# Attention with probabilities in two 16-bit planes: four DMA transposes per block in place of TensorE transposes

## The chip, the cores and the metric

The kernel runs on one core of a Trainium2 chip. The metric is device time in microseconds (us). Three timed runs of the kernel before gave 1548.31, 1543.1 and 1545.7 us, median 1545.7. Engines are named as in the profile: PE (TensorE, matmuls), PEld (its weight loads), DVE (VectorE), ACT (ScalarE), POOL (GpSimd), and SP, which issues the DMAs.

## The reference, cut to what matters

Two layers of attention and feed-forward; the change touches only the attention of the first layer. Batch is 8, with 256 own and 256 context positions, width 512, 16 query heads and 4 key/value heads of 128.

```python
q = rms_norm((x @ wq), q_norm_w)          # 16 heads; x has been layer-normalised
k = rms_norm((x @ wk), k_norm_w); v = x @ wv
k_ctx = rms_norm(h_ctx_kv @ wk_ctx, k_norm_w); v_ctx = h_ctx_kv @ wv_ctx
q = q * cos + rotate_half(q) * sin;  k = k * cos + rotate_half(k) * sin
k_full = concat([k_ctx, k]); v_full = concat([v_ctx, v])   # each repeated for 4 query heads
p = softmax(mask(q @ k_full.T / sqrt(128)))                # causal over own positions
out = (p @ v_full) @ wo
```

## The kernel before, in words

Attention is 64 blocks. Block i is one batch (i // 8), one key/value head (i // 2 % 4) and one half of its 128-query tiles (i % 2); it holds four query heads. An even block sees 384 keys (three tiles of 128), an odd one 512 (four tiles), so `width(i)` is 384 or 512 and `tiles_in(i)` is 3 or 4. A group is an even and an odd block that share keys and values. "Unit" u is one half (context for even, own for odd u, but for the first two) of the keys and values of group u // 2; unit i + 2 is computed during block i.

Precision is kept by splitting values into a high part and the rest: every product is three matmuls, high by high, low by high, high by low. In one block, in the order of the data: PE multiplies queries and keys into score banks (`pe_s`); DVE adds the mask, scales and takes the negative row maximum (`dve_ev`, L877); ACT takes the exponential and its row sum (`act_exp`, L617); DVE inverts the sums (`dve_ri`, L885); POOL multiplies by them (`pool_norm`, L1135); PE transposes the probabilities per tile of keys, four 128x128 each (`pe_p_turn`, L408); ACT copies the transposed bank as the high part (L609), DVE subtracts for the low part (L862); PE multiplies with the values (`pe_pv`, L421); ACT and DVE split the result into `OT` (L625, L912) and SP stores it (L282).

Beside that runs the preparation of later blocks. Keys and values of unit i + 2: PE (`pe_kv`, L338), ACT squares (`act_k_sq`), DVE adds epsilon (`dve_k_ss`, L800), POOL takes the power -0.5 (`pool_k_rs`, L1106), DVE multiplies (`dve_k_n`, L807), for own keys POOL applies the rotation in four instructions (`pool_k_rope`, L1113 to L1117), PE transposes (`pe_k_turn`), ACT and DVE split into `kT` (L575/L577, `dve_k_lo` L817/L819). Queries of block i + 2 go through `pe_q` (L368), `dve_q` (L841 to L843), `pool_q_add` (L1123), `pool_q_rs` (L1129), `pe_q_turn`, L601 and L855. Once per batch, in its blocks 4 to 6, context and x of the next batch are split, normalised (`dve_ln_a` L778 to L782, `dve_ln_b` L788) and transposed.

The order on each engine is written out by hand (`pe_even`, `pe_odd` and their counterparts); engines meet by counting semaphores, and each engine runs its list strictly in order. So a wait in a list holds all behind it. The first scores of an even block wait for the keys of its group (`kt_lo`, set by `dve_k_lo`) and its queries (`qt_lo`).

After attention PE multiplies with `wo` (`pe_y`, L1356) and the feed-forward follows. Its hidden values are already transposed by DMA (`sp_h_turn`, L1288): a 128x1024 16-bit tile per DMA.

## Time and profile before

| | value |
|---|---|
| profiled execution, its own time | 1547.26 us |
| its span | 1546.0 us, 26210 instructions |
| median of three timed runs | 1545.7 us |
| busy: PE, PEld, DVE, ACT, POOL | 96%, 75%, 74%, 62%, 45% of the span |
| granted clock, mean | 0.993 |
| attention, steady part | from about 100 to 860 us |

The page shows one profiled execution. Busy times are unions over an engine's instructions; matmuls are pipelined, so the time that one takes in a row of matmuls is the distance of the starts (0.23 us for 512 columns), not its own duration (about 0.39 us). An idle time is put down to what released it.

### The profile page before, as it was taken

The numbers are of one execution on the slowest core, as the hardware profiler recorded it, in microseconds if no ns is written. First come the engines' busy times: TensorE is split into PE (matmuls) and PEld (weight loads), VectorE is DVE, ScalarE is ACT, GpSimd is POOL, SyncE is SP. The second block draws the span as 40 slices with busy tenths as digits, with TensorE's granted clock in tenths as the row PEclk, the third lists the DMA queues.
The fourth block names the chain that finished last, engine by engine and source line by source line (L and its number), as shares of the span: only waits on it lengthen the run. The fifth ranks groups of instructions, "written<-read, shape, count | busy, mean of one in ns | idle before, by whom it ended". The sixth has DMA issues, their size and how long they took to land. (4 is left out here: it accounts for less than half of the span.)

```text
span 1546.0 us, 26210 instructions
## 1 busy us (share of the span) xinstructions
PE 1488.8 (96%) x8644; PEld 1165.6 (75%) x8644; DVE 1137.2 (74%) x2966; ACT 959.3 (62%) x2470; POOL 692.1 (45%) x832
## 2 busy tenths in 40 slices
PE   7899999999999999999999999999998899999988
...
GB/s 281 28 42 55 42 69 42 42 69 42 56 56 42 69 42 42 69 42 56 57 190 177 263 288 292 260 248 261 260 210 203 99 9 54 56 49 42 28 14 28
DMA packets 84327, 165.09 MB, mean 107 GB/s; under 512 B 39392, under 2 KB 39520, under 8 KB 82784
## 3 DMA queue, kind: packets, MB, share of 16 engines
...
HBM read 113.05 MB, written 41.94 MB: 100 GB/s over the span
## 5 line engine op out<-in xcount | busy, mean ns | idle before, releaser
L617 ACT ACTIVATE Pt<-Pt,small 128x384 f32<-128x384 f32 (+1 forms) x256 | 172.7, 682 | 106.1 <-DVE small L877 106.0
L368 PE MATMUL bank<-wq,xT 128*128 128x512 f32 x768 | 206.7, 404 | 1.0 <-DVE wq L772 1.0
L421 PE MATMUL bank<-PT,vv 128*128 128x512 f32 x672 | 199.6, 405 | 4.7 <-DVE PT L862 3.8
L1135 POOL TENSOR_SCALAR Pt<-Pt,small 128x384 f32<-128x384 f32 (+1 forms) x256 | 164.0, 653 | 79.0 <-DVE small L885 78.9
L877 DVE CUSTOM_DVE_ANT_0 Pt<-quad,mask,small 128x384 f32<-128x384 f32 (+1 forms) x256 | 171.6, 679 | 30.7 <-PE quad L398 29.4
L1356 PE MATMUL bank<-wq,ot 128*128 128x512 f32 x768 | 182.1, 395 | 1.5 <-DMA ot<-ot_scratch 1.5
L862 DVE TENSOR_TENSOR PT<-quad,PT 128x512 fp32r<-128x512 f32 x224 | 153.6, 686 | 37.9 <-ACT PT L609 37.5
L1356 PEld LDWEIGHTS bank<-wq,ot 128*128 128x128 f32 x768 | 143.9, 188 | 33.7 <-DMA ot<-ot_scratch 2.2
L368 PEld LDWEIGHTS bank<-wq,xT 128*128 128x128 f32 x768 | 136.8, 189 | 26.4 <-DVE wq L772 2.3
L1123 POOL TENSOR_TENSOR t<-t 128x512 f32<-128x512 f32 x64 | 83.6, 1306 | 144.1 <-DVE t L843 144.1
L421 PEld LDWEIGHTS bank<-PT,vv 128*128 128x128 f32 x672 | 116.4, 189 | 28.9 <-DVE PT L862 10.2
L1653 POOL TENSOR_TENSOR cl<-cl,fixed 128x1 f32<-128x1 f32 x16 | 8.8, 550 | 276.8 <-DVE cl L1537 276.8
L609 ACT CAST PT<-quad 128x512 fp32r<-128x512 f32 x224 | 128.7, 590 | 6.4 <-PE quad L408 6.4
L408 PE MATMUL quad<-fixed,Pt 128*128 128x128 f32 x896 | 129.0, 272 | 0.9 <-POOL Pt L1135 0.9
L408 PEld LDWEIGHTS quad<-fixed,Pt 128*128 128x128 f32 x896 | 109.2, 140 | 24.3 <-POOL Pt L1135 2.2
L625 ACT CAST OT<-bank 128x512 fp32r<-128x512 f32 x64 | 37.5, 587 | 138.1 <-PE bank L421 138.1
L2539 POOL TENSOR_TENSOR bhw<-bh,lnw 128x512 f32<-128x512 f32 x64 | 81.7, 1277 | 81.9 <-DVE bh L2327 81.9
L396 PE MATMUL quad<-kT,qT 128*128 128x384 f32 (+1 forms) x256 | 99.5, 389 | 2.2 <-DVE small L877 0.8
L1129 POOL TENSOR_TENSOR small<-small,fixed 128x4 f32<-128x4 f32 x64 | 66.1, 1033 | 72.3 <-DVE small L849 72.2
L338 PE MATMUL bank<-wkc,cT 128*128 128x256 f32 x744 | 97.2, 287 | 0.6 <-issue 0.6
L338 PEld LDWEIGHTS bank<-wkc,cT 128*128 128x128 f32 x744 | 91.0, 191 | 8.2 <-DVE vv L828 7.0
L338 PE MATMUL bank<-wkv,xT 128*128 128x256 f32 x744 | 96.5, 286 | 0.0
...
## 6 DMA issues: line engine op xcount, KB each, us to landing
...
```

What stands on the lines that cost most here:

```text
L338: ins = pe.matmul(kv_bank(u)[:, t * 256:t * 256 + 256], src[i][:, k, t * 128:t * 128 + 128], w[j][:, g, k, :], start=(n == 0), stop=(n == 11))
L368: ins = pe.matmul(bQ[:], xT[p][:, k, qt * 128:qt * 128 + 128], wq[j][:, g, k, :], start=(part == 0 and k == 0), stop=(part == 2 and k == 3))
L396: pe.matmul(bank[:, 0:n], qh, kh, start=True, stop=False)
L408: ins = pe.transpose(bP[k % 2][:, h * 128:h * 128 + 128], Pt[i % 2][:, h, kt * 128:kt * 128 + 128], idf[:])
L421: ins = pe.matmul(bO[:], vv[x][:, bg % 2, kt, :], PT[y][:, k % 2, :], start=(kt == 0 and n == 0), stop=(kt == tiles_in(i) - 1 and n == 2))
L609: act.copy(PT[0][:, k % 2, :], bP[k % 2]).then_inc(f["pt_hi"], 1)
L617: act.activation(p, p, ACT.Exp, bias=nm[:, i % 2, h:h + 1], scale=-1.0, accum_out=sm[:, i % 2, h:h + 1]).then_inc(f["s_exp"], 1)
L862: dve.tensor_tensor(PT[1][:, k % 2, :], bP[k % 2], PT[0][:, k % 2, :].bitcast(F32), ALU.subtract).then_inc(f["pt_lo"], 1)
L877: dve.tensor_tensor_reduce(Pt[i % 2][:, h, 0:n], bS[h % 2][:, 0:n], mask[:, 512 - n:512], scale=cq[:, i % 2, h:h + 1], scalar=3.0e38, op0= ...
L1123: pool.tensor_tensor(t1[:], t1[:], t2[:], ALU.add).then_inc(f["q_add"], 1)
L1135: pool.tensor_scalar(p, p, ri[:, i % 2, h:h + 1], 1.0, ALU.mult, ALU.mult).then_inc(f["p_n"], 1)
L1356: ins = pe.matmul(y_bank(n)[:], ot[:, c % 4, i, k * 128:k * 128 + 128].bitcast(F32R), wo[j][:, g, k, :], start=(g == 0 and k == 0 and q == ...
```

## The change

Scores use three banks instead of two (`bank_s`), and the fourth bank of `quad`, once used for transposed probabilities, holds the projections of the even units. The exponentials stay in one buffer `E`. POOL writes the normalised probabilities, times 2 to the 15, as a 16-bit high plane and DVE writes the 16-bit rest beside it; four DMA transposes per block (two heads by two planes) bring them to `PT`. Values are 16-bit planes too, scaled by a factor `sig` per head that is worked out once per batch from sums of squares (`act_c_square`, `pe_scale`, `dve_scale`, `pool_scale`); results are multiplied by `unsig` when they leave PSUM. ACT instead of DVE multiplies the keys (`act_k_n`), POOL instead of DVE applies the layer norm to x (`pool_ln`). The orders of all engines are written anew, one list for even and odd blocks.

```diff
-    bS = [quad[:, 0, :], quad[:, 1, :]]
-    bP = [quad[:, 2, :], quad[:, 3, :]]
+    bS = [quad[:, j, :] for j in range(3)]
...
-    vv = [sb(st, f"vv{j}", [128, 2, 4, 128], F32R) for j in range(2)]
+    vv = sb(st, "vv", [128, 2, 2, 4, 128], F16)
...
-    Pt = [sb(st, "Pt0", [128, 4, 384], F32), sb(st, "Pt1", [128, 4, 512], F32)]
+    E = sb(st, "E", [128, 4, 512], F32)
+    PT = [sb(st, "PT0", [128, 24, 128], F16)]
...
+    planes = sb(st, "planes", [128, 2, 2048], F16)
+    PT.append(sb(st, "PT1", [128, 32, 128], F16))
...
-        return bO if u in (0, 2) else bK
+        return bO if u == 2 else bK if u % 2 else quad[:, 3, :]
...
+    def sp_p_turn(i, p, x):
+
+        n = tiles_in(i)
+        if p == x == 0:
+            after(sp, f["pv_mm"], i - 1)
+        sp.wait_ge(f[("p_n", "p_lo")[x]], 4 * i + 2 * p + 2)
+        sp.dma_start_transpose(PT[i % 2][:, 4 * n * x + 2 * n * p:4 * n * x + 2 * n * p + 2 * n, :],
+                               planes[:, x, 2 * p * width(i):2 * p * width(i) + 2 * width(i)]).then_inc((t_hi, t_lo)[x], 16)
...
+            if i >= 2:
+                p = i - 2
+                sp.wait_ge(f["o_lo"], p + 1)
+                sp.dma_start(ot_dram[2 * (p // 8) + p % 2, p // 2 % 4], OT[:].bitcast(F32)).then_inc(f["ot0"], 16)
...
+            if i < NBLK:
+                for half in range(2):
+                    for x in range(2):
+                        sp_p_turn(i, half, x)
...
-        bank = bS[h % 2]
+        bank = bank_s(i, h)
         if h == 0:
             pe.wait_ge(f["kt_lo"], 2 * bg + 2)
             pe.wait_ge(f["qt_lo"], i + 1)
...
-        after(pe, f["s_ev"], 4 * i + h - 1)
+        if h == 1 and i and scaled(i - 1):
+            pe.wait_ge(f["v_scale"], 3 * scales(i - 1)[0] + 2)
+        after(pe, f["s_ev"], 4 * i + h - 2)
...
-    def pe_p_turn(i, kt):
-        if not 0 <= i < NBLK or kt >= tiles_in(i):
-            return
-        k = tile_of(i, kt)
-        if kt == 0:
-            pe.wait_ge(f["p_n"], 4 * i + 4)
-        after(pe, f["pt_lo"], k - 1)
-        for h in range(4):
-            ins = pe.transpose(bP[k % 2][:, h * 128:h * 128 + 128],
-                               Pt[i % 2][:, h, kt * 128:kt * 128 + 128], idf[:])
-        ins.then_inc(f["pt_mm"], 1)
...
+    def pe_scale(i):
+
+        k, b, lo, n = scales(i)
+        bank = bank_s(i, 2)
+        pe.wait_ge(f["v_sq"], squares(k))
+        pe.wait_ge(f["s_ev"], 4 * i + 3)
+        after(pe, f["v_scale"], 3 * k)
+        for j in range(2):
+            pe.matmul(bank[:, 384:384 + n], ones[:], w_sq[:, j, lo:lo + n], start=(j == 0), stop=(j == 1))
+        for j in range(2):
+            ins = pe.matmul(bank[:, 388:389], ones[:], c_sq[:, j:j + 1], start=(j == 0), stop=(j == 1))
+        ins.then_inc(f["v_scale"], 1)
+
+    def pe_pv(i, part):
+        if i < 0:
+            return
+        n = tiles_in(i)
+        x, y = ((0, 0), (1, 0), (0, 1))[part]
+        if part == 0:
+            pe.wait_ge(f["v_lo"], max(2 * (i // 2) + 2, 3))
             after(pe, f["o_lo"], i)
-        for n, (x, y) in enumerate(PRODUCTS):
-            ins = pe.matmul(bO[:], vv[x][:, bg % 2, kt, :], PT[y][:, k % 2, :],
-                            start=(kt == 0 and n == 0), stop=(kt == tiles_in(i) - 1 and n == 2))
-        ins.then_inc(f["pv_mm"], 1)
+            pe.wait_ge(t_hi, 32 * (i + 1))
+        if part == 2:
+            pe.wait_ge(t_lo, T_LO + 32 * (i + 1))
+        heads = PT[i % 2][:].rearrange("p (x h k) q -> p x h k q", x=2, h=4)
+        for kt in range(n):
+            ins = pe.matmul(bO[:].rearrange("p (h q) -> p h q", h=4), vv[:, x, i // 2 % 2, kt, :], heads[:, y, :, kt, :],
+                            start=(part == 0 and kt == 0), stop=(part == 2 and kt == n - 1))
+        if part == 2:
+            ins.then_inc(f["pv_mm"], 1)
...
         act.wait_ge(f["kt_lo"], u + 1)
-        after(act, f["pv_mm"], 7 * (bg - 1))
-        act.copy(vv[0][:, bg % 2, 2 * own:2 * own + 2, :], kv4(u)[:, 1]).then_inc(f["v_hi"], 1)
+        act.wait_ge(f["v_scale"], 3 * (min(bg, 3) if bg < 4 else bg // 4 + 3) if bg else 3)
+        after(act, f["pv_mm"], 2 * (bg - 1))
+        act.activation(vv[:, 0, bg % 2, 2 * own:2 * own + 2, :], kv4(u)[:, 1], ACT.Copy,
+                       scale=sig[:, bg // 4 % 2, bg % 4:bg % 4 + 1]).then_inc(f["v_hi"], 1)
...
+    def act_k_n(u):
+        if u >= NU:
+            return
+        act.wait_ge(f["k_rs"], u + 1)
+        after(act, f["kt_mm"], u)
+        for t in range(2):
+            ins = act.activation(kn[:, t], kv4(u)[:, 0, t], ACT.Copy, scale=krs[:, t:t + 1])
+        ins.then_inc(f["k_n"], 1)
...
+    def act_c_square(c):
+        b, t = divmod(c, 2)
+        act.wait_ge(f["c_hi"], c + 1)
+        if c in (2, 3):
+            act.wait_ge(f["v_scale"], 7)
+        act_square(c if b == 0 else 8 + c, cT[0][:, :, t * 128:t * 128 + 128], c_sq[:, t:t + 1])
...
-    def dve_k_n(u):
-        if u >= NU:
-            return
-        dve.wait_ge(f["k_rs"], u + 1)
-        after(dve, f["kt_mm"], u)
-        dve.tensor_tensor(kn, kv4(u)[:, 0], krs[:, 0:2].unsqueeze(2).broadcast_to((128, 2, 128)),
-                          ALU.mult).then_inc(f["k_n"], 1)
...
+        vh, vl = (vv[:, j, bg % 2, 2 * own:2 * own + 2, :] for j in range(2))
         dve.wait_ge(f["v_hi"], u + 1)
-        dve.tensor_tensor(vl, kv4(u)[:, 1], vh.bitcast(F32), ALU.subtract).then_inc(f["v_lo"], 1)
+        dve.scalar_tensor_tensor(vl, kv4(u)[:, 1], sig[:, bg // 4 % 2, bg % 4:bg % 4 + 1], vh,
+                                 ALU.mult, ALU.subtract).then_inc(f["v_lo"], 1)
...
-    def dve_p_lo(i, kt):
-        if not 0 <= i < NBLK or kt >= tiles_in(i):
-            return
-        k = tile_of(i, kt)
-        dve.wait_ge(f["pt_hi"], k + 1)
-        dve.tensor_tensor(PT[1][:, k % 2, :], bP[k % 2], PT[0][:, k % 2, :].bitcast(F32),
-                          ALU.subtract).then_inc(f["pt_lo"], 1)
+    def dve_p_lo(i, h):
+
+        dve.wait_ge(f["p_n"], 4 * i + h + 1)
+        if h == 0:
+            after(dve, t_lo, T_LO + 32 * i if i else 0)
+        dve.scalar_tensor_tensor(plane(i, 1, h), E[:, h, 0:width(i)], ri[:, i % 2, h:h + 1], plane(i, 0, h),
+                                 ALU.mult, ALU.subtract).then_inc(f["p_lo"], 1)
...
         dve.wait_ge(f["s_exp"], 4 * i + 2 * p + 2)
-        dve.reciprocal(ri[:, i % 2, 2 * p:2 * p + 2], sm[:, i % 2, 2 * p:2 * p + 2]).then_inc(f["s_ri"], 1)
+        r = ri[:, i % 2, 2 * p:2 * p + 2]
+        v.did(dve.reciprocal(r, sm[:, i % 2, 2 * p:2 * p + 2]))
+        v.settle()
+        dve.tensor_scalar(r, r, FULL, None, ALU.mult).then_inc(f["s_ri"], 1)
```

The new lists of PE, DVE and POOL, cut to what a plain block runs:

```diff
+    def pe_step(i):
+        pe_s(i, 0)
+        pe_s(i, 1)
+        pe_kv(i + 2)
+        pe_s(i, 2)
+        pe_s(i, 3)
+        pe_q_turn(i + 1)
+        for part in range(3):
+            pe_q(i + 2, part)
+        pe_pv(i - 1, 0)
+        pe_pv(i - 1, 1)
+        pe_k_turn(i + 2)
+        pe_pv(i - 1, 2)
...
+    def dve_step(i):
+        dve_ev(i, 0)
+        dve_ev(i, 1)
+        dve_o_lo(i - 2)
+        dve_v_lo(i + 1)
+        dve_q_ve(i + 1)
+        dve_ri(i, 0)
+        dve_last(i, 0)
+        dve_ev(i, 2)
+        dve_k_ss(i + 2)
+        dve_p_lo(i, 0)
+        dve_ev(i, 3)
+        dve_p_lo(i, 1)
+        dve_ri(i, 1)
+        dve_q_lo(i + 1)
+        dve_p_lo(i, 2)
+        dve_p_lo(i, 3)
+        if i % 8 == 5 and i + 3 < NBLK:
+            dve_ln_a(2 * (i // 8) + 2)
+            dve_ln_a(2 * (i // 8) + 3)
+        dve_last(i, 1)
+        dve_k_lo(i + 2)
+        dve_q(i + 2)
...
+    def pool_ln(m):
+        t, x = m % 2, x_slot(m)
         pool.wait_ge(f["ln_var"], m + 1)
-        pool.tensor_tensor(rs[:, t:t + 1], ve[:, t:t + 1], half[:, 0:1], ALU.pow).then_inc(f["ln_rs"], 1)
+        g_.did(pool.tensor_tensor(rs[:, t:t + 1], ve[:, t:t + 1], half[:, 0:1], ALU.pow))
+        g_.settle()
+        pool.tensor_scalar(x, x, mv[:, 2 * t:2 * t + 1], rs[:, t:t + 1], ALU.subtract, ALU.mult).then_inc(f["ln_x"], 1)
...
     def pool_norm(i, h):
-        p = Pt[i % 2][:, h, 0:width(i)]
         if h % 2 == 0:
             pool.wait_ge(f["s_ri"], 2 * i + h // 2 + 1)
-        pool.tensor_scalar(p, p, ri[:, i % 2, h:h + 1], 1.0, ALU.mult, ALU.mult).then_inc(f["p_n"], 1)
+        if h == 0:
+            after(pool, t_hi, 32 * i)
+        pool.tensor_scalar(plane(i, 0, h), E[:, h, 0:width(i)], ri[:, i % 2, h:h + 1], 1.0,
+                           ALU.mult, ALU.mult).then_inc(f["p_n"], 1)
...
+    def pool_step(i):
+            pool_q_add(i + 1)
+            pool_q_rs(i + 1)
+        pool_norm(i, 0)
+        pool_norm(i, 1)
+        pool_k_rs(i + 2)
+        if i % 2:
+            pool_k_rope(i + 2)
+        pool_norm(i, 2)
+        pool_norm(i, 3)
+        if i >= 57:
+            pool_wo(i - 57)
```

**PE, from the second pair of score heads of an odd block to the next block, before.** L398 is the end of the scores, L408 transposes probabilities, L421 multiplies with the values, L380 and L352 transpose queries and keys, L368 projects queries.

```order
L398 MATMUL quad<-kT,qT 128x512
L408 MATMUL quad<-fixed,Pt 128x128 x4
L421 MATMUL bank<-PT,vv 128x512 x3
L380 MATMUL bank<-fixed,t 128x128 x4
L368 MATMUL bank<-wq,xT 128x512 x8
L421 MATMUL bank<-PT,vv 128x512 x3
L352 MATMUL bank<-fixed,kk 128x128 x2
L368 MATMUL bank<-wq,xT 128x512 x4
L408 MATMUL quad<-fixed,Pt 128x128 x8
L396 MATMUL quad<-kT,qT 128x384
```

**The same place after the change.** L448 scores, L430 and L402 the transposes of queries and keys, L418 projects queries, L476 multiplies with the values.

```order
L448 MATMUL quad<-kT,qT 128x512
L430 MATMUL bank<-fixed,t 128x128 x4
L418 MATMUL bank<-wq,xT 128x512 x12
L476 MATMUL bank<-PT,vv 128x512 x6
L402 MATMUL bank<-fixed,kk 128x128 x2
L476 MATMUL bank<-PT,vv 128x512 x3
L446 MATMUL quad<-kT,qT 128x384
```

The transposes of probabilities are gone, and the product with the values stands in two runs behind the projection of queries, with the keys' transpose between them.

**DVE, the second half of an odd block, before.** L800 prepares the keys' scale, L877 takes scores (with a row for its accumulator), L807 scales keys, L862 makes the low part of a transposed tile, L885 inverts sums, L855 and L817 split queries and keys.

```order
L800 TENSOR_SCALAR small<-small 128x2 [waits k_sq]
L877 ISA Pt,small<-quad,mask,small 128x512 [waits s_mm]
L877 ISA small 128x1
L807 TENSOR_TENSOR kk<-bank,small 128x256 [waits kt_mm,k_rs]
L877 ISA Pt,small<-quad,mask,small 128x512 [waits s_mm]
L877 ISA small 128x1
L862 TENSOR_TENSOR PT<-quad,PT 128x512 [waits pt_hi]
L885 RECIPROCAL small<-small 128x2 [waits s_exp]
L855 TENSOR_TENSOR qT<-bank,qT 128x512 [waits qt_hi]
L817 TENSOR_TENSOR kT<-bank,kT 128x256 [waits kt_hi]
```

**The same place after the change.** L869 takes scores, L787 prepares the keys' scale, L856 makes the low plane of a head, L878 and L880 invert and scale the sums, L849 and L796 split queries and keys.

```order
L869 ISA E,small<-quad,mask,small 128x512 [waits s_mm]
L869 ISA small 128x1
L787 TENSOR_SCALAR small<-small 128x2 [waits k_rs,k_sq]
L856 SCALAR_TENSOR_TENSOR planes<-E,small,planes 128x512 [waits x_first,p_n]
L869 ISA E,small<-quad,mask,small 128x512 [waits s_mm]
L869 ISA small 128x1
L856 SCALAR_TENSOR_TENSOR planes<-E,small,planes 128x512 [waits p_n]
L878 RECIPROCAL small<-small 128x2 [waits s_exp]
L880 TENSOR_SCALAR small<-small 128x2 [waits v_step]
L849 TENSOR_TENSOR qT<-bank,qT 128x512 [waits qt_hi]
L856 SCALAR_TENSOR_TENSOR planes<-E,small,planes 128x512 [waits p_n] x2
L796 TENSOR_TENSOR kT<-bank,kT 128x256 [waits kt_hi]
```

The keys' scale (L787) now stands behind the third head of scores instead of ahead of it, the low planes read `E` and `planes`, and the last two stand right ahead of the keys (L796). POOL's list keeps its order in an odd block: two heads, the keys' scale, the four instructions of the rotation, two heads.

## Rows read from the trace of the kernel before

**Rows 1.** Page: busy time (share of the span) and instructions of each engine.
```profile
PE 1488.8 (96%) x8644; PEld 1165.6 (75%) x8644; DVE 1137.2 (74%) x2966; ACT 959.3 (62%) x2470; POOL 692.1 (45%) x832
```

**Rows 2.** Windows: start:end us, length, busy us per engine, PEclk, DMA share, GB/s.
```profile
core 0: us, PE busy (x) PEld busy (x) DVE busy (x) ACT busy (x) POOL busy (x), PEclk, DMA share, GB/s
100.00:860.00 760.00, 754.81 (x4610) 659.31 (x4610) 571.81 (x1460) 482.14 (x1641) 425.13 (x557) 1.00 0.19 70
```

**Rows 3.** Timeline of SP: start us, us, queue, line, operation, count.
```profile
129.79 78.29 SPq L282 DMA_DIRECT2D ot_scratch<-OT  x7
...
233.89 78.30 SPq L282 DMA_DIRECT2D ot_scratch<-OT  x7
```

**Rows 4.** Timeline of PE over a pair of blocks: start us, us, line, count.
```profile
439.71 0.48 PE L396 MATMUL quad<-kT,qT 128*128 128x512 f32 x1
...
440.48 0.60 PE L408 MATMUL quad<-fixed,Pt 128*128 128x128 f32 x4
...
440.84 3.11 PE L338 MATMUL bank<-wkv,xT 128*128 128x256 f32 x24
...
443.79 0.86 PE L421 MATMUL bank<-PT,vv 128*128 128x512 f32 x3
...
444.49 0.40 PE L396 MATMUL quad<-kT,qT 128*128 128x512 f32 x1
...
465.24 0.48 PE L396 MATMUL quad<-kT,qT 128*128 128x512 f32 x1
```

**Rows 5.** Timeline of PE in the next stage, 16-bit matmuls of 512 columns.
```profile
884.50 0.38 PE L1385 MATMUL quad<-wkv_h,xq 128*128 128x512 bf16 x1 [1.45 <-DVE wkc_h L2691]
884.72 0.38 PE L1385 MATMUL quad<-wkc_h,xq 128*128 128x512 bf16 x1
```

**Rows 6.** Groups of instructions: line, shapes, count | busy us, mean ns | idle, releaser.
```profile
L408 PE MATMUL quad<-fixed,Pt 128*128 128x128 f32 x896 | 129.0, 272 | 0.9 <-POOL Pt L1135 0.9
...
L862 DVE TENSOR_TENSOR PT<-quad,PT 128x512 fp32r<-128x512 f32 x224 | 153.6, 686 | 37.9 <-ACT PT L609 37.5
...
L885 DVE RECIPROCAL small<-small 128x2 f32<-128x2 f32 x128 | 20.5, 160 | 2.0 <-ACT Pt L617 1.2
```

**Rows 7.** One line of the program: durations in ns min/median/max.
```profile
L2712 DVE SCALAR_TENSOR_TENSOR wkv_h<-wkv_f,small,wkv_h x3: 1285/1285/1285, 852.3 to 885.1; 128x1024 bf16<-128x1024 f32 x3
```

**Rows 8.** Timeline of DVE and POOL at the start of the stage.
```profile
39.49 2.17 POOL L1135 TENSOR_SCALAR Pt<-Pt,small 128x384 f32<-128x384 f32 x2
...
40.00 1.21 DVE L772 TENSOR_TENSOR wq<-wq_in,wq 128x1024 fp32r<-128x1024 f32 x1
```

**Rows 9.** Timeline of POOL in the steady part.
```profile
442.96 1.37 POOL L1135 TENSOR_SCALAR Pt<-Pt,small 128x512 f32<-128x512 f32 x2 [0.33 <-DVE small L885]
...
444.90 0.71 POOL L1106 TENSOR_TENSOR small<-small,fixed 128x2 f32<-128x2 f32 x1 [0.58 <-DVE small L800]
...
446.55 0.47 POOL L1113 TENSOR_TENSOR kb<-kk,tab 128x128 f32<-128x128 f32 x1 [0.94 <-DVE kk L807]
...
448.94 1.36 POOL L1135 TENSOR_SCALAR Pt<-Pt,small 128x512 f32<-128x512 f32 x2
...
456.51 1.14 POOL L1135 TENSOR_SCALAR Pt<-Pt,small 128x384 f32<-128x384 f32 x2
```

**Rows 10.** Timeline of DVE, the end of the same block.
```profile
451.06 0.42 DVE L817 TENSOR_TENSOR kT<-bank,kT 128x256 fp32r<-128x256 f32 x1 [1.69 <-ACT kT L575]
...
452.66 0.41 DVE L828 TENSOR_TENSOR vv<-bank,vv 128x256 fp32r<-128x256 f32 x1
```

**Rows 11.** The DMA transposes of the next stage: issue ns; and us to landing.
```profile
L1288 SPq DMA_TRANSPOSE wkc_h<-hh x32: 1231/1282/3930, 897.0 to 1171.5; - x32
...
DMA to landing us min/median/max: 3.1/3.8/7.4
```

**Rows 12.** Groups of instructions that stand in or beside the chain once per batch or block.
```profile
L778 DVE BATCH_NORM_STATS2 small<-stg 128x6 f32<-128x512 f32 x14 | 9.6, 687 | 0.9 <-DMA stg<-in_x 0.9
...
L1140 POOL TENSOR_TENSOR wq<-wq_in,wq 128x1024 fp32r<-128x1024 f32 x8 | 19.3, 2414 | 1.8 <-ACT wq L630 1.8
```

524 lines of the change are left out of this document (177 added, 347 removed).

## The prediction

> **What bounds the kernel now.** I read the page's busy line first, then the windows, then the timelines of PE, DVE, POOL and SP over two blocks. The busy line [rows 1] is a mean over stages: PE 96%, DVE 74%, POOL 45%. In the steady part of attention [rows 2] PE is busy 754.81 of 760 us, so there PE's instruction list is the time; DVE has 571.81, ACT 482.14, POOL 425.13, and the clock is granted in full. The stores of results [rows 3] come back at the same place of the batch every 233.89 - 129.79 = 104.1 us, which is 13.0 us per block. PE's timeline [rows 4] gives one pair of blocks without the extras of a batch: 465.24 - 439.71 = 25.53 us. Four of these are 102.1; the other 2.0 are what a batch adds. So a gain must come off PE's list, and it lasts only as long as no other engine's list, or a loop through several, becomes longer than PE's.
>
> **What leaves PE's list.** Four transposes take 440.84 - 440.48 = 0.36 us [rows 4]; a pair has seven such groups, 2.5 us. Over the kernel 896 are removed [rows 6]. The product with the values keeps its 21 matmuls per pair: three take 444.49 - 443.79 = 0.70 us [rows 4], 0.233 each; 16-bit ones of 512 columns start 884.72 - 884.50 = 0.22 us apart [rows 5], so 0.3 us go. A pair on PE alone is 25.53 - 2.5 - 0.3 = 22.7 us, 11.35 per block. If nothing else bound, 32 pairs would give 32 x 2.8 = 90 us.
>
> **What the others get.** DVE's load per block is 571.81/760 x 13.0 = 9.8 us. It loses 3.5 subtractions of 0.686 [rows 6], 2.4 us, and the multiplication of the keys; it gets four low planes, two multiplications of the inverse sums (each about the 0.16 of the reciprocal [rows 6], and each after a wait for the reciprocal's end). The trace has no subtraction of this kind at 512 columns. At 1024, with the same mix of types and both tensors in SBUF, one takes 1.285 us [rows 7]: half of that, 0.64, is the lower bound and 1.285 the upper; since a fixed part doesn't double, I take 0.75 for 512 columns and a distance of 0.70 to the next, near the 0.686 from PSUM. So DVE stays at about 9.9 us per block: nothing for a block of 13, but 87% of 11.35. ACT loses the copies of 3.5 tiles and gets two short scalings of keys and, once per batch, two squares; with 482 of 760 us before, it doesn't bound, and its edits cost nothing outside the places named below. The scale factors of the values are a few small instructions once per batch, and I put them at nothing (up to 1 us per batch).
>
> The four DMA transposes: the next stage has the same ones, 128x1024 in 16 bits; SP needs 1.28 us for each and they land 3.8 us after issue, 7.4 at most [rows 11]. Four are 5.1 us of SP per block, three quarters of that width in even blocks, beside one store: SP has room. The high plane's last pair is issued right after the last POOL head; PE reads it some 8 us into the next block. The low plane's last transpose is issued at the end of the block and must have landed before the first low plane of the next block is written, about 6 us later. With 3.8 us it is hidden with over 2 us to spare. The queues behind it on SP (the store, the loads of x and context) have slack of several us.
>
> **The new loop.** What is late next is a chain over POOL and DVE in the odd block, since the first scores of the following even block wait for the keys that DVE splits at the very end of its list, behind the fourth low plane. Count from the odd block's first score matmul. Three heads of at most 0.77 and the key/value products, 443.79 - 440.84 = 2.95 [rows 4], bring the third head at 5.3. DVE takes it (0.69, the shape of L862) and only then prepares the keys' scale: 6.1. Behind it stand, in this order of need: the rest of POOL's second head (0 to 0.7; I take 0.5), the keys' power 0.71, ACT's scaling of keys about 0.5, the rotation 448.94 - 446.55 = 2.39, POOL's third and fourth head 1.36 [rows 9], a low plane 0.70, the keys' subtraction 0.42 [rows 10], and 0.2 for the semaphores: 12.8 at least. In the block before, the same scale was ready ahead of the third head, and rotation and heads were done by 450.30 [rows 9], where DVE still had time.
>
> DVE's low planes and POOL's instructions also meet at SBUF. At the start of the stage [rows 8] two POOL heads of 384 columns take 2.17 us, where they take 1.14 elsewhere [rows 9]: DVE's subtraction of two SBUF tensors runs from 40.00 to 41.21, and the second head, due to start at 40.06, is done at 39.49 + 2.17 = 41.66, 0.45 behind the end of DVE's instruction, which is about one head's own 0.57. So the second head stood still while DVE's ran. The new low planes are of that kind (E and planes both in SBUF), four per block, while POOL writes the heads; before, the second operand came from PSUM. I therefore add them to POOL's chain: 6.1 + 0.5 + low plane 0.70 + power 0.71 + low plane 0.70 + rotation 2.39 + two heads 1.36 + two low planes 1.40 + keys 0.42 + 0.2 = 14.5 us (ACT's scaling lies beside the second low plane). Bounds of the meeting: nothing (12.8) and full exclusion (14.5); the row is that of the full one, so I take 14.5.
>
> The Trainium skill says the same in its page "SBUF — State Buffer", section "Who interferes with whom": a DVE instruction with two SBUF inputs and a GpSimd instruction that reads SBUF exclude one another for the whole instruction. By that rule the loop is the 14.5, and without it 12.8; the trace agrees for the pair in rows 8.
>
> The even block has 0.575 per POOL head, no rotation, and no scores that wait for its keys: it stays on PE's 11.3. A pair is 14.5 + 11.3 = 25.8, against 25.53: 32 x 0.3 = +9 us. PE idles 3 us in each odd block, what the removed transposes had taken.
>
> Once in seven batches' turns, two statistics of x stand between the last low plane and the keys (i % 8 == 5). One is 0.687 [rows 12] and two short ones of about 0.17 with waits: 1.05, two 2.1, all in the loop now, where before DVE had idle time. In the block before, ACT's two squares make the exponentials late: 0 to 1.2 us, I take 0.6. 7 x 2.7 = +19 us. In the last blocks POOL splits `wo`, 2.414 us each, seven of them inside [rows 12], and DVE sums `w1`; in the odd ones they stand beside the loop: -5 to +20 us with the head of the kernel, I take +4. The sum is +32 us on the profiled execution's own 1547.26 (span 1546.0, 1.3 around it): 1579. The median of the runs shown is 1.6 below that execution, so 1577.
>
> **Rivals.** First, low planes and POOL don't meet, or only in part. For it: DVE's 40.00 row is not itself stretched, and one instance is thin. Against it: 2.17 against 1.14. Then a pair is 12.8 + 11.3 = 24.1: 32 x -1.4 = -46, with the same +19 and +0: 1520, faster. The point from which the sign turns is an odd block of about 13.6 us. Second, my chain has slack I don't see (the third head or the keys' scale come earlier) and PE stays the bound: 1547 - 90 = 1457, up to 1490 with the batches' extras. For it: PE's 99% now and the 90 us off its list; against it: the order of DVE's list. Third, the transposes land late, since they share the queues with the stores: at 7.4 us each the first low plane of an even block starts 1.2 us later and that of an odd one 0.4: 32 x 1.6 = +51 more, 1628. For it: the 7.4 seen; against it: those were at a much larger DMA load than the 0.19 here [rows 2], to which the transposes add. That the change doesn't do what it says is no case: the order shows the transposes gone from PE.
>
> **How the numbers follow.** The loop at 14.5 has 0.60, no meeting 0.20, PE-bound 0.13, late transposes 0.07. The likeliest gives 1577, its own range 1548 to 1608 (the odd block within 0.9 us, the tail). Less than 2 in 10 is left out by 1508 to 1612, which holds the loop, the case without meeting and its neighbourhood. Within 0.3% (4.6 us) is about what a measurement of this kernel can't tell from no change. Faster by more: all of PE-bound, 0.16 of no meeting, 0.04 of the loop, 0.33; within: 0.06; slower: 0.61.
>
> **What would show it.** The distance of the stores at one place of the batch: 108.5 us against 104.1 (loop), about 102 (no meeting), 93 (PE-bound). In an odd block PE's scores of the next block wait for DVE's key subtraction (now L796) with about 3 us in total, part of it at the keys' transpose; PE busy in the steady part near 88%. POOL heads beside a low plane last longer than 0.69, or low planes longer than 0.75. The 16-bit product spaced at 0.22. Transposes landing in under 6 us. I am wrong if PE is over 96% busy between 100 and 860 us, or if the scores wait for something else than the keys.

## The result, and the profile after

The changed kernel takes 1653.1 us (median; 1648.2 to 1654.5), the kernel before 1546.1: a ratio of 1.069, 95% interval 1.066 to 1.072. Slower, as forecast, but by 107 us and not by 31. The profiled executions span 1650.8 and 1546.0 us. The line numbers below are those of the changed kernel.

The page's busy line and one row of the windows answer to [rows 1, 2]:

```profile
PE 1447.5 (88%) x7777; PEld 1071.8 (65%) x7820; DVE 1213.8 (74%) x3076; ACT 926.2 (56%) x2422; POOL 769.4 (47%) x888
```
```profile
100.00:860.00 760.00, 662.39 (x3604) 527.43 (x3603) 575.61 (x1433) 408.82 (x1461) 450.66 (x559) 0.93 0.50 115
```

PE is busy 662 of 760 us, 87% (forecast 88), so PE's list no longer sets the time. Two numbers were not in the forecast: a granted clock of 0.93 in place of 1.00, and a DMA share of 0.50 in place of 0.19. The odd block's chain, rows of PE, DVE, POOL and ACT in one timeline, answers to [rows 4, 9, 10]:

```profile
406.80 0.58 PE L446 MATMUL quad<-kT,qT 128*128 128x512 f32 x1
...
412.83 0.17 DVE L787 TENSOR_SCALAR small<-small 128x2 f32<-128x2 f32 x1
412.91 1.12 DVE L856 SCALAR_TENSOR_TENSOR planes<-E,small,planes 128x512 f16<-128x512 f32 x1
...
413.46 1.14 POOL L1029 TENSOR_TENSOR small<-small,fixed 128x2 f32<-128x2 f32 x1
...
414.63 0.74 DVE L856 SCALAR_TENSOR_TENSOR planes<-E,small,planes 128x512 f16<-128x512 f32 x1
414.64 0.63 ACT L629 ACTIVATE kk<-bank,small 128x128 f32<-128x128 f32 x2 [0.87 <-POOL small L1029]
...
415.34 0.47 POOL L1036 TENSOR_TENSOR kb<-kk,tab 128x128 f32<-128x128 f32 x1 [0.74 <-ACT kk L629]
...
417.68 1.36 POOL L1059 TENSOR_SCALAR planes<-E,small 128x512 f16<-128x512 f32 x2
418.41 1.83 DVE L856 SCALAR_TENSOR_TENSOR planes<-E,small,planes 128x512 f16<-128x512 f32 x2 [0.90 <-POOL planes L1059]
420.17 0.41 DVE L796 TENSOR_TENSOR kT<-bank,kT 128x256 fp32r<-128x256 f32 x1
...
420.63 0.44 PE L446 MATMUL quad<-kT,qT 128*128 128x384 f32 x1 [1.79 <-DVE kT L796]
...
431.56 0.58 PE L446 MATMUL quad<-kT,qT 128*128 128x512 f32 x1
```

This is the forecast loop, link by link: keys' scale (L787), POOL's power (L1029), ACT's scaling of the keys (L629), rotation (from L1036), POOL's last heads, two low planes (L856), the keys' subtraction (L796), the next scores. It takes 420.63 - 406.80 = 13.8 us, forecast 14.5; the even block behind it takes 431.56 - 420.63 = 10.9 us, forecast 11.3. In one link the forecast was right by luck: it had POOL stand still there for the second low plane, and POOL waited 0.74 us for ACT's scaling instead. The low planes and the DMA transposes, as groups, answer to [rows 6, 7, 11]:

```profile
L856 DVE SCALAR_TENSOR_TENSOR planes<-E,small,planes 128x512 f16<-128x512 f32 x106 | 98.7, 950 | 28.9 <-POOL planes L1059 28.8
L856 DVE SCALAR_TENSOR_TENSOR planes<-E,small,planes 128x384 f16<-128x384 f32 x108 | 72.3, 688 | 9.9 <-POOL planes L1059 9.9
```
```profile
L291 SPq DMA_TRANSPOSE PT<-planes x256: 1209/1232/5587, 42.6 to 972.4; - x128
...
DMA to landing us min/median/max: 2.7/3.0/11.1
```

A low plane of 512 columns takes 0.74 us with POOL idle (at 414.63), as forecast, but 0.95 in the mean of this stage; at 412.91, where POOL's second head is still running, it takes 1.12. The transposes land in 3.0 us (median; the slowest took 11.1).

**Where the 105 us are.** Once per block POOL adds the two halves of the rotated queries (L1046). The starts of its 64 rows are a clock by block, and split each span. A sum stands at the head of POOL's list and is for the queries of the next block, so blocks named by this clock begin and end a little later than on PE:

```
us                         before   after   more
to the 1st sum              22.8     28.8    +6.0
1st to 9th                 104.5    134.2   +29.7
9th to 49th (5 batches)    521.5    550.0   +28.5   (104.3 -> 110.0 a batch)
49th to 64th               196.6    230.6   +34.0
behind the 64th            700.7    707.3    +6.6
```

The first and last stretches lose 76 us and the five batches in the middle 28.5. Within a batch the odd blocks 1 and 3 take 13.27 us (before 13.20) and block 2 takes 11.49 (12.33): a plain pair is 24.8 us, a little shorter than the 25.5 of before. Block 0 takes 13.68 us and block 4 13.32 (12.33 and 15.53). Blocks 5 and 6, where the rows of the next batch are normalized and transposed, go from 24.5 to 31.7 us together, and that is more than the whole loss of a batch.

**The lower clock.** PE's rows, and below them the window's:

```profile
391.51 0.44 PE L402 MATMUL bank<-fixed,kk 128*128 128x128 f32 x2 [1.75 <-POOL kk L1040]
...
394.38 0.45 PE L446 MATMUL quad<-kT,qT 128*128 128x384 f32 x1 [1.79 <-DVE kT L796]
...
395.56 4.52 PE L388 MATMUL quad<-wkc,cT 128*128 128x256 f32 x24
...
417.76 0.44 PE L402 MATMUL bank<-fixed,kk 128*128 128x128 f32 x2 [0.45 <-POOL kk L1040]
...
421.81 3.03 PE L388 MATMUL quad<-wkc,cT 128*128 128x256 f32 x24
```
```profile
395.00:400.00 5.00, 5.00 (x30) 5.00 (x29) 3.12 (x11) 2.33 (x12) 3.42 (x4) 0.66 0.61 171
```

PE waited 1.75 and 1.79 us, and then 24 matmuls took 4.52 us where [rows 4] have 3.11. The granted clock of these 5 us is 0.66: part of them ran at 1.2 GHz and part at 2.4. This is at the start of a batch. Inside it, in the loop shown above, PE waited 0.45 and 1.79 us, and the same 24 matmuls took 3.03 us: a plain pair doesn't lose the clock.

**Block 5 of a batch** (rows of several engines; the next batch's statistics are L771, its normalization L1023):

```profile
468.98 1.83 DVE L856 SCALAR_TENSOR_TENSOR planes<-E,small,planes 128x512 f16<-128x512 f32 x2 [0.90 <-POOL planes L1059]
470.74 0.68 DVE L771 BATCH_NORM_STATS2 small<-stg 128x6 f32<-128x512 f32 x1
...
472.58 2.08 POOL L1023 TENSOR_SCALAR stg<-stg,small 128x512 f32<-128x512 f32 x1
472.75 0.41 DVE L796 TENSOR_TENSOR kT<-bank,kT 128x256 fp32r<-128x256 f32 x1
...
473.22 0.69 PE L446 MATMUL quad<-kT,qT 128*128 128x384 f32 x1 [3.80 <-DVE kT L796]
...
475.32 2.08 POOL L1023 TENSOR_SCALAR stg<-stg,small 128x512 f32<-128x512 f32 x1
```

The two statistics are in the loop, 472.75 - 470.74 = 2.0 us, as forecast. Then come two things that were not: POOL has the normalization, and the matmul behind PE's wait of 3.80 us lasts 0.69 us instead of 0.44.

**Block 57**, in the last blocks (SP, DVE, ACT and PE):

```profile
843.18 8.97 SPq L291 DMA_TRANSPOSE PT<-planes  x4
852.20 0.58 SPq L256 DMA_DIRECT2D wkv_f<-in_w  x1
...
854.24 0.48 SPq L251 DMA_DIRECT2D wq_in<-in_wo  x1
```
```profile
860.26 1.22 DVE L884 TENSOR_REDUCE small<-wkv_f 128x1 f32<-128x1024 f32 x1 [5.07 <-DMA wkc_f<-in_w]
...
863.24 1.04 ACT L668 CAST wq<-wq_in 128x1024 fp32r<-128x1024 f32 x1 [7.51 <-DMA wq_in<-in_wo]
...
868.00 0.69 PE L402 MATMUL bank<-fixed,kk 128*128 128x128 f32 x2 [7.04 <-POOL kk L1040]
```

SP issues in order. The four transposes of block 56 wait for DVE's low planes, so the weights' loads behind them go out at 852.20. DVE waits 5.07 us for them ahead of the third head's eviction, ACT 7.51 us for the output weights ahead of its scaling of the keys, and PE 7.04 us for these keys.

### The profile page after: what moved, and what is told of

Read it like the earlier page. It is cut to its first block and busy times, and to the rows that moved or that the text cites. A ratio compares the mean times of both kernels' runs of the same rounds, so it can differ in the third digit from the quotient of the medians.

```text
span 1650.8 us, 24906 instructions
## 1 busy us (share of the span) xinstructions
PE 1447.5 (88%) x7777; PEld 1071.8 (65%) x7820; DVE 1213.8 (74%) x3076; ACT 926.2 (56%) x2422; POOL 769.4 (47%) x888
## 5 line engine op out<-in xcount | busy, mean ns | idle before, releaser
L856 DVE SCALAR_TENSOR_TENSOR planes<-E,small,planes 128x384 f16<-128x384 f32 (+1 forms) x256 | 219.4, 876 | 46.1 <-POOL planes L1059 46.0
L869 DVE CUSTOM_DVE_ANT_0 E<-quad,mask,small 128x384 f32<-128x384 f32 (+1 forms) x256 | 169.8, 676 | 54.3 <-PE quad L448 54.3
L418 PE MATMUL bank<-wq,xT 128*128 128x512 f32 x768 | 199.9, 409 | 8.4 <-ACT wq L553 6.1
L655 ACT ACTIVATE E<-E,small 128x384 f32<-128x384 f32 (+1 forms) x256 | 171.2, 675 | 44.8 <-DVE small L869 44.7
L1059 POOL TENSOR_SCALAR planes<-E,small 128x384 f16<-128x384 f32 (+1 forms) x256 | 161.9, 645 | 62.4 <-DVE small L880 62.4
L446 PE MATMUL quad<-kT,qT 128*128 128x384 f32 (+1 forms) x256 | 110.8, 433 | 78.9 <-DVE kT L796 78.5
L476 PE MATMUL bank<-PT,vv 128*128 128x512 f16 x672 | 169.5, 386 | 0.0
L418 PEld LDWEIGHTS bank<-wq,xT 128*128 128x128 f32 x768 | 142.8, 193 | 38.8 <-issue 6.2
L1046 POOL TENSOR_TENSOR t<-t 128x512 f32<-128x512 f32 x64 | 83.0, 1297 | 152.2 <-DVE t L837 152.2
L388 PE MATMUL quad<-wkc,cT 128*128 128x256 f32 x720 | 117.3, 333 | 0.0
L388 PEld LDWEIGHTS quad<-wkc,cT 128*128 128x128 f32 x720 | 116.8, 245 | 0.0
L476 PEld LDWEIGHTS bank<-PT,vv 128*128 128x128 f16 x672 | 61.6, 99 | 68.6 <-issue 19.3
L448 PE MATMUL quad<-kT,qT 128*128 128x384 f32 (+1 forms) x256 | 100.2, 392 | 0.0
L447 PE MATMUL quad<-kT,qT 128*128 128x384 f32 (+1 forms) x256 | 99.7, 390 | 0.0
L388 PEld LDWEIGHTS bank<-wkv,xT 128*128 128x128 f32 x744 | 93.5, 189 | 2.5
```

Of the source, the lines that this page charges most:

```text
L388: ins = pe.matmul(kv_bank(u)[:, t * 256:t * 256 + 256], src[i][:, k, t * 128:t * 128 + 128], w[j][:, g, k, :], start=(n == 0), stop=(n == 11))
L418: ins = pe.matmul(bQ[:], xT[p][:, k, qt * 128:qt * 128 + 128], wq[j][:, g, k, :], start=(part == 0 and k == 0), stop=(part == 2 and k == 3))
L446: pe.matmul(bank[:, 0:n], qh, kh, start=True, stop=False)
L447: pe.matmul(bank[:, 0:n], ql, kh, start=False, stop=False)
L448: pe.matmul(bank[:, 0:n], qh, kl, start=False, stop=True).then_inc(f["s_mm"], 1)
L476: ins = pe.matmul(bO[:].rearrange("p (h q) -> p h q", h=4), vv[:, x, i // 2 % 2, kt, :], heads[:, y, :, kt, :], start=(part == 0 and kt == ...
```

## The experiments

The kernel before, timed beside these, had 1544.7 to 1547.0 us.

**One: the keys ahead of two low planes.**

```diff
+        if i % 2:
+            dve_k_lo(i + 2)
         dve_p_lo(i, 2)
         dve_p_lo(i, 3)
```

> One edit in DVE's list: in odd blocks the keys' low plane (L796) goes ahead of the low planes of heads three and four. Nothing is left out. Theory A (the time per pair of blocks is a loop, and these two low planes are in it): in the block from 406.80 us of the changed kernel's trace DVE ended them at 420.24 and only then made the keys' low plane, although the rotated keys were there at 417.70 and the transpose and its copy want about 0.9 us; the first scores of the next block come 1.5 us earlier, 1.5 x 32 pairs = -48 us, to about 1605 us, and the wait of PE on the keys' low plane falls from some 2 us to under 1 us a pair. Rival B (DVE and POOL are simply full, so an order changes nothing): within 5 us of 1653. Rival C (the low planes that come later delay the transposes): PE waits for the transposes by DMA before the values' products instead, and the time is within 15 us of 1653.

Measured: 1610.2 us (ratio 1.043, 1.041 to 1.045). Theory A holds in kind; B and C don't. DVE's and PE's rows of an odd block's end:

```profile
424.31 0.42 DVE L796 TENSOR_TENSOR kT<-bank,kT 128x256 fp32r<-128x256 f32 x1 [1.12 <-ACT kT L593]
424.65 1.41 DVE L856 SCALAR_TENSOR_TENSOR planes<-E,small,planes 128x512 f16<-128x512 f32 x2
```
```profile
424.79 0.44 PE L446 MATMUL quad<-kT,qT 128*128 128x384 f32 x1 [0.27 <-DVE kT L796]
```

The wait for the keys is 0.27 us instead of 1.79, and a batch takes 104.6 us instead of 110.0. The time is near A's 1605, but the gain isn't spread as A had it: a plain pair falls by 0.8 us (24.76 to 23.94) and not by 1.5, while block 0 falls from 13.68 to 11.28 and block 4 from 13.32 to 11.54. The next run shortens these two blocks as well, with the loop as it was, so part of this gain is the clock.

**Two: filler in PE's waits.**

```diff
+        if i % 2 == 0 and i > 1:
+            pe_fill(i, 9)
         pe_s(i, 0)
...
+        if i % 2 and i < 62:
+            pe_fill(i + 1, 4)
         pe_k_turn(i + 2)
```

> PE gets work of no use in its two waits of each pair: nine 16-bit matmuls of 512 columns (some 1.9 us) ahead of the first scores of an even block and four (0.85 us) ahead of the keys' transpose of an odd one. Nothing else changes. Theory K (after these waits TensorE was granted the lower clock, and its matmuls at 1.2 GHz lie on the path): the granted clock comes back to about 1.00 over the attention, the keys' and values' products after a wait take 2.95 us and not 4.4, and 5 us a batch plus some 15 us in the first and the last blocks are saved, -50 us, to about 1603 us. Rival B (the lower clock falls in time that PE has anyway, the loop through POOL and DVE sets the period): granted clock 1.00, and the time within 10 us of 1653.

Measured: 1617.9 us (1.047, 1.046 to 1.049), the window of the batches first for the changed kernel, then for this one:

```profile
100.00:760.00 660.00, 573.47 (x3131) 456.40 (x3130) 504.00 (x1254) 357.56 (x1278) 393.74 (x489) 0.93 0.50 113
```
```profile
100.00:760.00 660.00, 633.41 (x3587) 480.26 (x3588) 520.43 (x1305) 369.35 (x1328) 405.51 (x506) 0.99 0.53 118
```

The clock is back at 0.99 and 35 us with it, by work that computes nothing: theory K, at two thirds of its size. The plain pair didn't move (13.26 and 11.55 us); the loop sets it at either clock. Block 0 of a batch fell from 13.68 to 11.59, block 6 from 13.73 to 12.68 and block 4 from 13.32 to 12.81. Of the 35 us, 18 are in the five batches, 6 in the first blocks and 10 in the last.

**Three: the keys' chain earlier.** On top of the first, in odd blocks:

```diff
+        if i % 2:
+            dve_k_ss(i + 2)
         dve_ev(i, 2)
...
+        if i % 2:
+            pool_k_rs(i + 2)
         pool_norm(i, 0)
```

> The edit of the first run and two more in odd blocks: the keys' sum of squares (L787) ahead of the third head's eviction and POOL's inverse root (L1029) ahead of the first two normalizations; the first low plane behind the fourth eviction. Nothing is left out. Theory A: the chain from the keys' squares to their rotation begins 0.7 us earlier too, so 2.2 us less a pair, about -70 us, to some 1583 us, and PE's wait for the rotated keys goes from 1.1 us to under 0.5 us. Rival B (lists are not the limit): as the first run or no better than 5 us from it. Rival C (the later normalizations make the transposes late): PE waits for the transposes, and the time is above the first run's.

Measured: 1605.3 us (1.039, 1.037 to 1.041), 5 us below the first where 22 were expected, so A's second part fails and B is right. An odd block went only from 13.05 to 12.73 us. Its rows on POOL and DVE say why:

```profile
336.65 1.36 POOL L1068 TENSOR_SCALAR planes<-E,small 128x512 f16<-128x512 f32 x2
...
337.37 2.04 DVE L856 SCALAR_TENSOR_TENSOR planes<-E,small,planes 128x512 f16<-128x512 f32 x2 [0.16 <-POOL planes L1068]
337.98 0.88 POOL L1045 TENSOR_TENSOR kb<-kk,tab 128x128 f32<-128x128 f32 x1
```

The power is early, but the two heads now stand between it and the rotation, and the rotation meets two low planes: its first step takes 0.88 us and not 0.47, the two low planes 2.04 and not 1.41.

**Four: POOL's heads cut.**

```diff
-        pool.tensor_scalar(plane(i, 0, h), E[:, h, 0:width(i)], ...
+        pool.tensor_scalar(plane(i, 0, h)[:, 0:16], E[:, h, 0:16], ...
```

> Left out: POOL's normalization into the high plane writes 16 of 384 or 512 columns from the third block on (the probabilities' high planes are not made); all waits, low planes and transposes stay. Theory A (POOL is in the loop, and it and DVE exclude each other while they read two operands from SBUF): L856 goes from 876 ns in the mean to 680 ns, POOL's inverse root and rotation start about 1.3 us earlier and DVE's last two low planes end 1 us earlier in each odd block: about 2.3 us a pair, -70 us, to some 1580 us. Rival B (PE at the lower clock is the limit): L856 shorter, but the time within 20 us of 1653. Rival C (PE's own list at full clock is reached): -90 us or more, PE over 96% busy from 100 to 860 us.

Measured: 1584.2 us (1.025, 1.023 to 1.027), theory A's 1580. The odd block falls to 12.05 us and a batch to 101.1. The low planes:

```profile
L856 DVE SCALAR_TENSOR_TENSOR planes<-E,small,planes 128x512 f16<-128x512 f32 x114 | 87.1, 784 | 15.3 <-POOL planes L1060 15.0
```

784 ns instead of 950, and in one odd block 0.75 and 0.75 us, with 1.42 for a pair that took 1.83. POOL's heads are in the loop, by their own time, by the meeting, or by both: the run doesn't separate the two. The mean over both widths fell from 876 to 742 ns where A had 680; POOL's power and rotation were left in.

**Five: the next batch's rows (block 5 and 6).** On the third; the statistics go ahead of the keys' subtraction, PE's transposes of rows behind the fourth head, ACT's copies behind the fourth exponential.

```diff
-        if turn:
-            pe_x_turn(2 * (i // 8) + 2)
         pe_kv(i + 2)
-        if turn:
-            pe_x_turn(2 * (i // 8) + 3)
         pe_s(i, 2)
         pe_s(i, 3)
+        if turn:
+            pe_x_turn(2 * (i // 8) + 2)
+            pe_x_turn(2 * (i // 8) + 3)
```

> The kernel with the keys' chain early in odd blocks (1605 us), and one more edit: LayerNorm's statistics of the next batch go ahead of the keys' low plane in block 5 of a batch (DVE is idle there for 1.8 us), and in block 6 PE transposes the next batch's rows behind the fourth score head instead of behind the second; ACT's and DVE's copies of them follow. Nothing is left out. Theory T: from block 5 to block 6 a batch takes 17.9 us from one queries' sum to the next, in all kernels so far, where other odd blocks take 12.8, because DVE makes the statistics behind its low planes, POOL normalizes the rows after that, and PE waits 3.9 us for them and then runs the keys' and values' products at the lower clock (5.3 us and not 2.95): this step falls to about 13.5 us, 4.4 x 7 = -31 us, to some 1574 us. Rival U (the rows' work has to be done by DVE and POOL somewhere and pushes another step as far): the step falls and block 6 or 7 grows by as much, within 8 us of 1605.

Measured: 1619.4 us (1.047, 1.045 to 1.049), 14 us worse than the third. Block 5 gave 1.9 us and block 6 took 3.5. PE's row:

```profile
467.68 1.09 PE L430 MATMUL bank<-fixed,t 128*128 128x128 f32 x4 [5.05 <-issue]
```

PE waits 5 us for the copies of the rows, which ACT has behind the scaling of keys and the fourth exponential. Theory T fails as built, and U's trade is what the blocks show, though U had the time within 8 us of 1605; run nine shows that it was the place of the copies.

**Six: the first blocks.** On the third; ACT's squares for the values' scale behind the first keys, and the queries' weights later on PE:

```diff
+        late = 1 <= i <= 4
-        for part in range(3):
+        for part in range(0 if late else 3):
             pe_q(i + 2, part)
...
+        for part in range(2 if late else 0):
+            pe_q(i + 2, part)
         pe_k_turn(i + 2)
+        if late:
+            pe_q(i + 2, 2)
```

> The kernel with the keys' chain early in odd blocks (1605 us), and the lists of the first blocks alone changed: ACT squares the contexts and weights for the values' scale behind its copies of the first keys instead of ahead of the queries' squares; POOL adds the second queries ahead of the first normalizations; in blocks 1 to 4 PE multiplies the queries' weights behind the first two parts of the values' product, and ACT and DVE split those weights earlier. Nothing is left out. Theory H (the first blocks are late by waits that the new lists made): PE's waits of 3.6 us for the summed queries at 44 us and of 2.9 us for the weights' high plane in blocks 2 and 4 go, with the lower clock behind them, and the first keys come 1.5 us earlier: -12 to -15 us up to the eighth block, to about 1592 us. Rival D (DVE is full in the first blocks, with weights' low planes and probabilities' low planes both on it): the waits move to other lines and under 4 us are won.

Measured: 1593.4 us (1.031, 1.029 to 1.032). The stretch from the 1st to the 9th sum goes from 128.2 to 118.7 us: theory H, but by one of its two waits. Blocks 2 and 4, which lost the wait for the weights (2.9 us), fell from 17.7 to 13.6 and from 19.3 to 14.6 us. The wait of 3.6 us for the summed queries gave way to one of 3.8 us for the weights (PE at 48.14), and from the 1st to the 3rd sum it stayed at 27 us.

**Seven: the last blocks.** On the third; `sp_w1` ahead of the transposes of blocks 56 and 58, and:

```diff
-        for q in {(57, 0): (0,), (57, 1): (1,), (58, 0): (2,), (58, 1): (3,), (59, 0): (4,), (59, 1): (5,),
-                  (60, 0): (6, 7)}.get((i, half), ()):
+        for q in {(57, 1): (0,), (58, 0): (1,), (58, 1): (2,), (59, 1): (3,), (60, 0): (4, 5),
+                  (60, 1): (6, 7)}.get((i, half), ()):
```

> The kernel with the keys' chain early in odd blocks (1605 us), and the last blocks alone changed: the sums of absolute values of the FFN's first weights go behind the keys' low plane in odd blocks and fall more to the even ones, their total is taken a block later, and SP issues the loads of those weights ahead of the transposes of blocks 56 and 58. Nothing is left out. Theory E (in blocks 57 and 59 DVE waits for the weights' transfer, 5.6 and 3.4 us, ahead of the third head's eviction, and the keys' chain starts behind it): these two blocks take 23.8 and 21.3 us and fall to about 13.5 and 14.5, -16 us or so, to about 1589 us. Rival M (the last blocks are long by the work of the weights itself, 8 x 1.21 us on DVE and 8 x 2.4 us on POOL): blocks 57 to 61 keep their sum within 5 us, and the time stays near 1601.

Measured: 1600.4 us (1.035, 1.033 to 1.037), 5 us below the third, a third of theory E's 16. Block 59 fell from 21.3 to 16.7 us, block 57 only to 21.0: ACT waited 5.91 us there for the output weights, whose load had stayed behind the transposes.

**Eight: five to seven together**, with their three diffs.

> All of the edits of the other three together on the kernel with the keys' chain early in odd blocks. Nothing is left out. If the causes are separate in place, their gains add: 1605 - 31 - 13 - 16 = about 1545 us, level with the kernel before. If they push each other (the last rows' transposes and the first weights share DVE), some 10 to 20 us of that are missing.

Measured: 1606.7 us (1.039, 1.036 to 1.041). Against the third, six had gained 12 us and seven 5, and five had lost 14; together they lose 1. About 1545 us was expected, or 1555 to 1565 if the edits push each other, and both fail. The gains are eaten by the fault of five.

**Nine: the same, mended.** The diff is cut: DVE's copies of the rows move with ACT's, and ACT's work on the queries' and output weights changes its place too.

```diff
         act_exp(i, 2)
+        if turn:
+            act_x_hi(2 * (i // 8) + 2)
+            act_x_hi(2 * (i // 8) + 3)
...
         act_exp(i, 3)
-        if turn:
-            act_x_hi(2 * (i // 8) + 2)
-            act_x_hi(2 * (i // 8) + 3)
...
-        if i in (56, 58, 60, 62):
-            sp_wo(i // 2 - 28)
...
+            if i in (56, 58, 60, 62):
+                sp_wo(i // 2 - 28)
             if i < NBLK:
                 for half in range(2):
```

> The combined kernel with four of its edits mended. In block 6 ACT and DVE copy the transposed rows right behind the third head (in the last run PE waited 5 us for these copies behind the second transpose); in block 0 ACT splits the queries' weights ahead of the third exponential; SP issues the loads of the output weights too ahead of the transposes of blocks 56 to 62 (ACT waited 5.9 us for one ahead of the third exponential of block 57), and ACT converts them behind the keys' chain in odd blocks. Nothing is left out. Theory S (each of these is a wait in an in-order list, and goes when the instruction is moved): against the 1605 us of the kernel with the keys' chain early, -13 us up to the eighth block, -14 us behind the 56th, and 3 us a batch (blocks 5 and 6 together 29 us instead of 32), -21 us: about 1557 us. Rival D (DVE and POOL are too full at these places): as the last combined run within 10 us, near 1600.

Measured: 1549.3 us (1.0026, 1.0013 to 1.0040): theory S, and more than it had (1557). Blocks 5 and 6 take 27.1 us together (32.0 in the third), a batch 98.9. The window:

```profile
100.00:760.00 660.00, 614.22 (x3539) 481.96 (x3538) 543.44 (x1416) 392.45 (x1441) 459.92 (x550) 1.00 0.58 131
```

In this window the clock is granted in full without any filler. PE still waits, but less in a row: at the start of a batch 1.49 us and then 0.38 (at 419.81 and 421.28), where the changed kernel had 1.75 and 1.79. In the first 100 us and from 760 to 900 the granted clock is still 0.86 and 0.89.

**Ten: filler in that kernel.**

```diff
+        if i % 2 and i < 62:
+            pe_fill(i + 1, 5)
         pe_k_turn(i + 2)
```

> The mended combined kernel, and five 16-bit matmuls of 512 columns of no use ahead of the keys' transpose of each odd block, where PE has waited 1.5 us. Theory K (the lower clock after these waits still costs): the granted clock goes from some 0.97 to 1.00 over the attention, and 5 to 10 us are won. Rival B (with the short waits left, the lower clock falls in time that PE has anyway): within 3 us of the run without them, or slower where the filler is longer than the wait.

Measured: 1549.7 us (1.0023, 1.0012 to 1.0035): rival B. With the clock at 1.00 over the batches there is nothing to give back there.

**Eleven: SP's list alone.** The changed kernel, and only this:

```diff
-        if i == 56 or i == 58:
-            sp_w1(i // 2 - 28)
-        if i in (56, 58, 60, 62):
-            sp_wo(i // 2 - 28)
...
+            if i == 56 or i == 58:
+                sp_w1(i // 2 - 28)
+            if i in (56, 58, 60, 62):
+                sp_wo(i // 2 - 28)
             if i < NBLK:
                 for half in range(2):
                     for x in range(2):
                         sp_p_turn(i, half, x)
```

> The changed kernel (1653 us) with one edit, in SP's list alone: the loads of the FFN's first weights and of the output weights go ahead of the four transposes of blocks 56, 58, 60 and 62 instead of behind them. Nothing is left out. Theory Q (SP issues in order, the transposes wait for DVE's low planes, and the loads behind them come so late that DVE and ACT wait for them at the head of the keys' chain): blocks 57 and 59 take 15 us or less instead of 23.1 and 21.4, -14 us or so, to about 1639 us. Rival M (the last blocks are long by the work of the weights itself): blocks 57 to 61 keep their sum within 4 us, and the time stays at 1653.

Measured: 1642.8 us (1.062, 1.060 to 1.064). SP's rows:

```profile
841.86 0.43 SPq L256 DMA_DIRECT2D wkv_f<-in_w  x1
...
844.19 0.70 SPq L251 DMA_DIRECT2D wq_in<-in_wo  x1
844.99 10.97 SPq L287 DMA_TRANSPOSE PT<-planes  x4
```

Block 57 goes from 23.1 to 17.2 us and block 59 from 21.4 to 16.6, 10 us over the last blocks: theory Q in kind, at 10 of its 14 us, without a change to what DVE and ACT do. They stay 3 to 4 us above the 13.4 of before, and Q had 15 us or less; what holds these 3 to 4 us wasn't tested.

**Twelve: the first keys.**

```diff
         act_w_hi(5)
+        act_k_n(0)
         act_q_sq(0)
         act_k_sq(1)
-        act_k_n(0)
```

> The mended combined kernel (1549.3 us), and one edit at its start: ACT scales the first keys ahead of the squares of the first queries instead of behind them and the second keys' squares. Nothing is left out. Theory F (the first blocks start 5.5 us later than before the change because the scaling, now ACT's and at 25.18 us, waits in ACT's list behind squares that wait for DVE's rotation, while POOL has had nothing to do for 5.1 us): POOL's rotation of the first keys starts near 22.5 us instead of 25.95, the first queries' sum near 25 instead of 28.25, and 3 us are won, to about 1546 us, level with the kernel before. Rival G (the weights' conversions set the first blocks): the sum moves and the second block does not; within 1 us of 1549.

Measured: 1546.9 us (1.0004, 0.9992 to 1.0016). The rotation of the first keys in run nine, and here:

```profile
25.95 0.45 POOL L1047 TENSOR_TENSOR kb<-kk,tab 128x128 f32<-128x128 f32 x1 [5.06 <-ACT kk L632]
```
```profile
22.10 0.46 POOL L1047 TENSOR_TENSOR kb<-kk,tab 128x128 f32<-128x128 f32 x1 [1.59 <-ACT kk L632]
```

Theory F holds: 22.10 for its 22.5, 1546.9 for its 1546. With this the kernel has the work of the changed one and the time of the one before: 106 us came back by the places of instructions alone. It doesn't beat it. Against before, the middle batches gain 26.6 us, and the stretch to the 9th sum loses 10.3, the one from the 49th to the 64th 9.3 and the rest 6.2.

## Why the prediction was wrong

- **PE's list, -90 us.** The list is shorter, as forecast. Batches of 98.9 us in run nine, against 104.3, show part of the gain once the waits are off; the 93 of a PE-bound batch was not reached by any run.
- **The loop, 25.8 us a pair.** The mechanism was right and is shown by runs one and four. Its size was 24.8: counted as in the forecast, from scores to scores, the odd block has 13.8 (14.5 forecast) and the even one 10.9 (11.3). The 0.7 us of the odd block are small pieces; the largest seen are that the power lay partly beside a low plane and that the last two low planes begin beside POOL's heads (both together end at 420.24, 2.56 us behind 417.68, where the forecast had 2.76). This term alone would have made the kernel faster, 32 x -0.77 = -25 us instead of +9. So that the kernel got slower, as forecast, is luck as far as this term goes: the loss came from terms that the forecast had small or not at all.
- **The meeting at SBUF.** It is there: 0.95 us against 0.74, a pair 1.83 against 1.41. Full exclusion (14.5) was too much for the whole chain, and no meeting (12.8) too little. My prices for the quiet plane (0.75) and for the transposes (3.8 us to landing, 3.0 measured) held; in the plain block measured, PE waits for keys and not for a transpose.
- **The batch's extras, 2.7 us.** The statistics took the 2.0 us forecast, but a batch has 110.0 - 4 x 24.76 = 11.0 us beside its pairs, where mine had 4.7. POOL's normalization and the copies of the rows were not priced: with the statistics moved and the copies earlier, blocks 5 and 6 fell from 32.0 to 27.1 us. How much belongs to each of these edits wasn't separated, except that with the copies late (run five) nothing was won. Of the 11.0 us, filler gives back 3.7 (run two), most of it in block 0.
- **The step that failed: "-5 to +20 us with the head of the kernel, I take +4".** The first and last stretches lost 76 us; with their share of pairs and batches the forecast had 13 there. I took the weights' work to stand beside the loop. It stands in the loop's lists: ACT's and DVE's instructions wait for transfers that SP issues behind waiting transposes (10 us, run eleven), and PE and ACT met the weights and squares in an order that made waits (10 us with run six, most of it by the wait of 2.9 us for weights; 3 us more, run twelve). Of the 76 us, 26 are still there in run twelve. I had written that SP has room, counting its busy time; what mattered was what its waits hold back.
- **A step that is missing: the clock.** All terms were at the full clock of [rows 2]. The waits that the loop makes in PE brought it down, and that cost 35 us (run two). It overlaps with the others: each edit that shortened PE's waits raised the clock as well.

Together: 76 instead of 13 in the first and last stretches, and 28.5 instead of 19.5 in the middle, are the 72 us between forecast and result. Open is what the last blocks' 9 us still are, and the loss behind the 64th sum, 5 to 13 us in the runs. In the changed kernel it lies between the first product with `wo` and the feed-forward's first transposes by DMA, 43 us before and 54 after (4 us come back later), and PE's and SP's rows there point the same way as run eleven:

```profile
961.08 12.68 SPq L291 DMA_TRANSPOSE PT<-planes  x4
...
975.86 2.43 SPq L1178 DMA_DIRECT2D ot<-ot_scratch  x3
```
```profile
971.68 5.04 PE L1277 MATMUL bank<-wq,ot 128*128 128x512 f32 x12 [5.48 <-POOL wq L1077]
...
983.55 8.60 PE L1277 MATMUL bank<-wq,ot 128*128 128x512 f32 x24 [4.11 <-DMA ot<-ot_scratch]
```

PE waits 5.48 us for POOL's split of `wo` and 4.11 us for results that SP reads back behind the last block's transposes. No run tested this.
